# Softmax sums of the second key head: ones-products on TensorE, or accumulating transfers into SBUF

## The chip, the cores and the metric

The kernel runs on one core of a Trainium2 chip. The metric is the device time of one execution in microseconds (us); a kernel's number is the median of several executions. The engines are named as in the profile: PE is TensorE's matmuls, PEld its weight loads, DVE is VectorE, ACT is ScalarE, POOL is GpSimd, SP is SyncE; SPq, ACTq and POOLq are their DMA-issuing instructions.

## What is computed

The input `x` has 8192 rows of 128 channels. A graph layer with the dense 8192 x 8192 matrix `adj` comes first, then a transformer block with causal attention over the 8192 rows (4 query heads of 32 channels, 2 key and value heads, each of which serves 2 query heads), then a mixture of 8 expert networks of which each row uses 2. Cut to what matters here:

```python
x = x + relu(A_norm @ (layernorm(x) @ W.T))          # graph stage, reads adj
h = rmsnorm(layernorm(x), ln1_w)
q, k, v = rotate(h @ wq.T), rotate(h @ wk.T), h @ wv.T
scores = q @ k.T / sqrt(32), causal                   # per query head
att = softmax(scores)                                 # exp(scores - shift) / sum over keys
y = att @ v
x1 = x0 + y @ wo.T                                    # then router, top 2 of 8 experts, result added
```

The part in question is the sum over keys in the softmax: for every query and head, the sum of `exp(scores - shift)` over all keys up to the query's own.

## The kernel before, in words

Three stages run one after the other. `graph_stage` streams `adj` from memory in transfers of 1 MB. `attention_stage` computes attention, the output projection, and the routing of the rows to experts. `expert_stage` runs the experts over the gathered rows and adds the result. The change is in `attention_stage` alone.

Attention works on 16 blocks of 512 queries (`T` = 0 to 15) and, for each, on the `T + 1` blocks of 512 keys that it may see. One pair of a query block and a key block is a **unit**; there are 16 x 17 / 2 = 136, numbered by `first_unit(T) + v`. Within block `T`, `v = 0` is the diagonal unit (masked, with narrower tiles), and `v = 1` to `v = T` are the full ones. A unit has four **chunks** (`j` = 0 to 3) of 128 keys, and in each chunk two **key heads** (`kv` = 0 and 1), each with two query heads.

The work of one chunk, and who does it:

- PE, `scores` (L1234): transposed scores of 128 keys by 2 x 512 queries into `ps_scores[kv]`, two products. There is one such bank pair for each key head, so `scores` for the next chunk waits until ACT has read the last.
- ACT, `exponentials` (L918): `probs[:, j, kv]` = exp of it, 128 x 1024 in float32, one instruction for each key head. `probs` has four chunks and two key heads, exactly one unit; so ACT writes chunk `j` of a unit over chunk `j` of the unit before, and waits until its readers are done: `chunk_used` (PE's products) for both heads, and `chunk_added` (POOL's additions) for key head 0.
- PE, `weigh` (L1245): weights times values into `ps_out`, in four column strips of 32, one for each query head.
- The softmax sums. For key head 0 POOL adds the chunk's `probs` to `chunk_sum` element by element (`add_chunk`, L783 and L786), and once for each query block PE sums `chunk_sum` over its partitions (`combine`, L1273). For key head 1 PE does it all: `add_weights` (L1255) multiplies `probs` of two chunks by a block of ones, in four column strips at once, and adds into `ps_sum`. It runs twice in a unit, after chunks 1 and 3 (after 2 and 3 in a diagonal one).
- PE, `gap`, called four times for each chunk: in a full unit it holds one `max_pass` (L1215), a product whose 128 x 512 result DVE reduces to a row maximum (`reduce_tile`, L958). It is the shift of the next query block, `T + 1`; block 15 has none to prepare. Two banks (`ps_max`) alternate, and a product waits until DVE is done with the one before the last (`bank_free`).

The order of PE's instructions is written out by hand in `unit_of_block`: the scores of chunk `j + 1` are issued ahead of the weighing of chunk `j`, with gaps between. Where a chunk is `paired` (odd, in a full unit), the scores of the two key heads are issued back to back and the gap that would stand between them comes after `weigh`.

Beside this the stage routes rows to experts. DVE, ACT and PE work on it in the gaps; POOL's part (`route`, called after each chunk) are two additions for each query block (L793, L798) and the **scatters** (`scatter_rows`, L810): indirect DMAs of 128 rows of 130 values (66 KB) from `batch_rows` to `scratch_slots`. One is issued after each chunk in units 25 to 32, 48 to 55, 90 to 97 and 128 to 133, 120 in all in 30 units; before it is issued, POOL waits until the scatter before has landed:

```python
                if earlier:
                    pool.wait_ge(rows_scattered, 16 * earlier)
```

All DMAs that POOL issues go to one queue, which the profile lists as q0. In the first 12 units ACT also issues large transfers that fill `scratch_slots` and `scratch_parts` (L860, L868).

Of the kernel before, what the change touches and what calls it, by code (L numbers as in the profile page):

```python
# [25 lines left out]
P = 128  # L26
C = 128
SUB = 4
BT = SUB * P
NH, NKV, HD = 4, 2, 32  # L30
NREP = NH // NKV
# [546 lines left out]
def attention_stage(nc, NB, dram, keep):  # L578
# [10 lines left out]
    PER_CHUNK = NKV  # L589
    EXPS = SUB * PER_CHUNK  # L590
# [10 lines left out]
    first_unit = lambda T: T * (T + 1) // 2  # L601
# [5 lines left out]
    for Rs in batches[:-1]:  # L607
# [4 lines left out]
        paces.append(1 if LAST - 1 in Rs else 2)  # L612
        scattered_at.append(routed_at[-1] + 4 * paces[-1])

    def preparing(unit):

        for R in range(LAST):
            if prepared_at[R] <= unit < prepared_at[R] + 3:
                yield R, unit - prepared_at[R]
# [24 lines left out]
    with ExitStack() as ctx:  # L644
# [4 lines left out]
        q_stack = sb("q_stack", [STACK, QBUF, NH, BT], F16)  # L649
        probs = sb("probs", [P, SUB, NKV, NREP, BT])  # L650
        chunk_sum = sb("chunk_sum", [P, NREP, BT])
        zeros = sb("zeros", [SHIFT_ROW, P], F16)
        even_and_odd = sb("even_and_odd", [P, P])
        unit_max = sb("unit_max", [P, TILES, NB + 1])
# [47 lines left out]
        exp_done = sem("exp_done")  # L702
        chunk_used = sem("chunk_used")
        chunk_added = sem("chunk_added")
        numerator_copied = sem("numerator_copied")
        sums_copied = sem("sums_copied")
        combined = sem("combined")
# [66 lines left out]
        def _(pool):  # L774
            def add_chunk(T, unit, j, diagonal):
# [8 lines left out]
                else:  # L784
                    pool.wait_ge(chunk_added, unit * SUB + j)
                    nc.gpsimd.tensor_tensor(chunk_sum[:, :, lo:], chunk_sum[:, :, lo:], weights, ALU.add  # L786
                                            ).then_inc(chunk_added, 1)

            def divide(R):
                pool.wait_ge(inverted, SUB * (R + 1))  # L790
                pool.wait_ge(numerator_copied, R + 1)
                here = attended[:, R * BT:(R + 1) * BT]
                nc.gpsimd.tensor_tensor(here, here, denominators[:, R % KEPT], ALU.mult).then_inc(block_divided, 1)  # L793
# [47 lines left out]
            for T in range(NB):  # L841
                for n, G in enumerate(units_of(T)):
                    for j in range(SUB):
                        add_chunk(T, first_unit(T) + n, j, n == 0)
                        route(first_unit(T) + n, j)
            divide(LAST)
            keep_residual(LAST)
# [3 lines left out]
        def _(act):  # L851
# [58 lines left out]
            def exponentials(unit, j, diagonal):  # L910
                lo = j * P if diagonal else 0
                for kv in range(NKV):
                    act.wait_ge(scores_ready, unit * EXPS + (PER_CHUNK * j + kv + 1))
                    if unit:
                        act.wait_ge(chunk_used, unit * SUB + (j - SUB + 1))
                        if kv == 0:
                            act.wait_ge(chunk_added, unit * SUB + (j - SUB + 1))
                    nc.scalar.activation(probs[:, j, kv, :, lo:], ps_scores[kv][:, :, lo:], ACT.Exp,  # L918
                                         scale=SCALE).then_inc(exp_done, 1)

# [277 lines left out]
        def _(pe):  # L1198
# [51 lines left out]
            def add_weights(j, diagonal):  # L1250
# [6 lines left out]
                                                start=False, stop=True, skip_group_check=True)  # L1257
                return last

            def clear_sums(T):  # L1260
                if T:
                    pe.wait_ge(sums_kept, T)
                nc.tensor.matmul(ps_sum[:], zeros[:], k_stack[0:SHIFT_ROW, 0, 0:BT], start=True, stop=True,
                                 skip_group_check=True)
# [67 lines left out]
            def unit_of_block(T, v):  # L1332
                unit, G, diagonal = first_unit(T) + v, units_of(T)[v], v == 0
                if diagonal:
                    pe.wait_ge(max_rounded, T + 1)
                    gap(T, v, 0)
                    gap(T, v, 1)
                    pe.wait_ge(shift_placed, T * 16 + 16)
                    for kv in range(NKV):
                        scores(T, unit, G, 0, kv, True)  # L1340
                for j in range(SUB):
                    paired = not diagonal and j % 2
                    for kv in range(NKV):
                        if j + 1 < SUB:
                            scores(T, unit, G, j + 1, kv, diagonal)
                        elif v < T:
                            scores(T, unit + 1, units_of(T)[v + 1], 0, kv, False)
                        if not (diagonal and j == 0) and not (paired and kv == 0):
                            gap(T, v, 4 * j + kv - bool(paired))
                    pe.wait_ge(exp_done, unit * EXPS + PER_CHUNK * (j + 1))  # L1350
                    if diagonal and j == 0 and T:
                        pe.wait_ge(numerator_copied, T)
                    weigh(G, j, diagonal)
                    if paired:
                        gap(T, v, 4 * j + 1)
                    gap(T, v, 4 * j + 2)
                    if diagonal and j == 2:
                        clear_sums(T)
                    if j in ((2, 3) if diagonal else (1, 3)):
                        add_weights(j if j % 2 else j - 1, diagonal).then_inc(chunk_used, 2)  # L1360
                    if diagonal and j == 0 and T:
                        combine(T - 1, lambda: gap(T, v, 3))
                    else:
                        gap(T, v, 4 * j + 3)
# [465 lines left out]
```

## Time and profile before

| | us |
|---|---|
| three runs, median (lowest to highest) | 4142.93 (4135.64 to 4162.34) |
| the profiled execution, own time | 4167.11 |
| its span in the profile | 4165.5 |
| PE busy in the span | 3452.7 (83%) |
| DVE busy | 2752.5 (66%) |
| POOL busy | 1638.8 (39%) |
| ACT busy | 1306.4 (31%) |
| mean granted TensorE clock, share of full speed | 0.911 |

The profiled execution is a single one; its own time is 24.2 us above the median of the three runs, and all durations of the trace are from it. The span is the profile's window from the first to the last instruction. Busy time counts instructions only, not waits; an engine's share over the whole span is a mean over three stages with different limits. The attention stage lies at about 1,500 to 3,680 us of the span.

### The profile page before, as it was taken

The page shows a single profiled execution, that of the slowest core. Times are in us where ns is not written, and L with a number is a line of the kernel's source. Part 1 is how long each engine was busy: PE and PEld are TensorE (multiplying, and loading weights), DVE is VectorE, ACT ScalarE, POOL GpSimd, SP SyncE. Part 2 cuts the span into 40 slices and gives each one's busy share as a digit, 9 for nine tenths or more (in the row PEclk, how much of TensorE's full clock was granted, in tenths as well). Part 3 has the DMA queues.
Part 4 walks back from the last instruction along what each step waited for, and adds up shares of the span by engine and source line. Part 5 has one row for each costly group of instructions (what it writes and reads, how often), then busy time and mean ns, then how long its engine had stood idle before and what let it go on. Part 6 is the DMA issues. An engine that isn't in the chain of part 4 may idle for free. (4 is left out here: it accounts for less than half of the span.)

```text
span 4165.5 us, 48116 instructions
## 1 busy us (share of the span) xinstructions
PE 3452.7 (83%) x16381; PEld 1324.3 (32%) x16381; DVE 2752.5 (66%) x3882; ACT 1306.4 (31%) x1635; POOL 1638.8 (39%) x1016
## 2 busy tenths in 40 slices
PE   1456899999999859987999899999899999839960
PEld 1233444444444312222222222222222222105540
DVE  8778887614344457777778878777777775326752
ACT  0000000000000014433444455454445455625640
POOL 1000000000000014544766486565478566844551
PEclk8567899999999969999999999999999999969985
DMA  9888998787888436500100000000000000012225
GB/s 372 347 346 346 345 344 319 288 292 284 296 296 291 169 123 236 181 10 5 33 13 6 12 21 8 10 1 10 1 23 9 6 1 6 12 54 65 75 65 181
DMA packets 165282, 572.71 MB, mean 137 GB/s; under 512 B 20193, under 2 KB 55786, under 8 KB 114550
## 3 DMA queue, kind: packets, MB, share of 16 engines
q1 hardware_dynamic: 91304, 457.35, 29.7%
q10 hardware_dynamic: 60432, 88.88, 6.0%
q0 software_dynamic: 13360, 24.03, 1.8%
q8 instruction: 113, 1.85, 0.2%
q14 instruction: 73, 0.60, 0.0%
HBM read 478.22 MB, written 90.57 MB: 137 GB/s over the span
## 5 line engine op out<-in xcount | busy, mean ns | idle before, releaser
L958 DVE TENSOR_REDUCE unit_max<-ps_max 128x1 f32<-128x512 f32 (+3 forms) x2176 | 1356.6, 662 | 424.2 <-PE ps_max L1215 306.6
L786 POOL TENSOR_TENSOR chunk_sum<-chunk_sum,probs 128x1024 f32<-128x1024 f32 (+1 forms) x528 | 1196.1, 2265 | 577.4 <-ACT probs L918 563.2
L918 ACT ACTIVATE probs<-ps_scores 128x1024 f32<-128x1024 f32 (+1 forms) x1088 | 1020.9, 984 | 1057.2 <-PE ps_scores L1234 858.4
L1215 PE MATMUL ps_max<-keep_k_stack,q_stack 96*128 96x512 f16 (+3 forms) x2176 | 762.1, 383 | 154.4 <-DVE unit_max L958 114.1
L1234 PE MATMUL ps_scores<-q_stack,keep_k_stack 97*128 97x512 f16 (+3 forms) x2176 | 616.1, 378 | 36.4 <-ACT probs L918 32.6
L1245 PE MATMUL ps_out<-probs,keep_v 128*32 128x512 f32 (+3 forms) x4352 | 567.2, 594 | 0.6 <-ACT probs L918 0.6
L314 DVE TENSOR_TENSOR partial_degree<-partial_degree,ring 128x2048 f32<-128x2048 f32 x240 | 550.0, 2292 | 7.1
L1215 PEld LDWEIGHTS ps_max<-keep_k_stack,q_stack 96*128 96x128 f16 x2176 | 182.2, 97 | 974.8 <-DVE unit_max L958 822.2
L497 PE MATMUL ps_gather<-ring,keep_attended 128*128 128x512 f32 x960 | 449.2, 630 | 22.1 <-DVE keep_attended L338 22.1
L512 PE MATMUL ps_gather_low<-ring,keep_attended 128*128 128x512 f32 x800 | 362.2, 609 | 1.4 <-DVE keep_attended L338 1.4
L277 POOL DMA_DIRECT2D scratch_lower<-lower x15 | 9.3, 618 | 815.7 <-ACT lower L416 815.7
L1234 PEld LDWEIGHTS ps_scores<-q_stack,keep_k_stack 97*128 97x128 f16 x2176 | 208.0, 99 | 325.0 <-ACT probs L918 112.4
L1255 PE MATMUL ps_sum<-probs,keep_ones_heads 128*32 128x512 f32 (+3 forms) x2176 | 295.1, 610 | 0.0
L497 PEld LDWEIGHTS ps_gather<-ring,keep_attended 128*128 128x128 f32 x960 | 193.3, 204 | 263.3 <-issue 263.3
L289 POOL DMA_DIRECT2D keep_k_stack<-k_hi x64 | 31.8, 497 | 577.2 <-DVEq L385 575.2
L1535 POOL DMA_INDIRECT scratch_parts<-moe_y_rows,moe_y_index x156 | 161.6, 1036 | 139.8 <-issue 70.0
L512 PEld LDWEIGHTS ps_gather_low<-ring,keep_attended 128*128 128x128 f32 x800 | 154.2, 196 | 184.5 <-issue 183.0
L481 PE MATMUL ps_gather_low<-ones,partial_degree 128*128 128x1 f32 x512 | 102.4, 334 | 115.9 <-DVEq L333 112.7
L1245 PEld LDWEIGHTS ps_out<-probs,keep_v 128*32 128x32 f32 x4352 | 86.1, 108 | 185.6 <-issue 168.3
L460 PE MATMUL ps_turn<-keep_ident,normed 128*128 128x128 f32 x128 | 25.0, 328 | 138.9 <-DVE normed L329 102.4
L481 PEld LDWEIGHTS ps_gather_low<-ones,partial_degree 128*128 128x128 f32 x512 | 101.1, 306 | 122.7 <-DVEq L333 115.4
L810 POOL DMA_INDIRECT scratch_slots<-batch_rows,keep_slot_index x120 | 118.5, 988 | 36.8 <-POOL chunk_sum L786 16.0
(232 smaller groups left out, 2709.7 us busy)
## 6 DMA issues: line engine op xcount, KB each, us to landing
ring<-in_adj SPq DMA_DIRECT2D x392, 1024.0 KB, 6.7
scratch_slots<-empty_rows ACTq DMA_DIRECT2D x16, 2080.0 KB, 7.4
scratch_parts<-empty_part ACTq DMA_DIRECT2D x8, 2048.0 KB, 7.6
moe_parts<-scratch_parts SPq DMA_DIRECT2D x64, 256.0 KB, 3.5
moe_x_rows<-scratch_slots SPq DMA_DIRECT2D x39, 260.0 KB
x_in<-in_x SPq DMA_DIRECT2D x16, 256.0 KB, 6.0
x_in<-in_x ACTq DMA_DIRECT2D x16, 256.0 KB, 9.9
cos<-in_cos ACTq DMA_DIRECT2D x16, 256.0 KB, 8.0
```

Source lines behind the costliest of these rows:

```text
L314: add = nc.vector.tensor_tensor(partial_degree[:], partial_degree[:], ring[:, g % R, :], ALU.add)
L481: last = nc.tensor.matmul(ps_degree[:, s:s + 1], partial_degree[:, c * BT + s * P:c * BT + (s + 1) * P], ones[:], start=(c == 0), stop=(c ...
L497: last = nc.tensor.matmul(ps_gather[:], support[:, g * SUB + c, :], ring[:, g % R, c * BT:(c + 1) * BT], start=(g == 0 and c == 0), stop=( ...
L512: last = nc.tensor.matmul(bank[:], support[:, g * SUB + c, :], ring[:, slot, c * BT:(c + 1) * BT], start=(start and c == 0), stop=True, sk ...
L786: nc.gpsimd.tensor_tensor(chunk_sum[:, :, lo:], chunk_sum[:, :, lo:], weights, ALU.add).then_inc(chunk_added, 1)
L918: nc.scalar.activation(probs[:, j, kv, :, lo:], ps_scores[kv][:, :, lo:], ACT.Exp, scale=SCALE).then_inc(exp_done, 1)
L958: nc.vector.tensor_reduce(unit_max[:, i, at:at + 1], bank[:, 0:width], AX_X, ALU.max).then_inc(bank_free, 1)
L1215: last = nc.tensor.matmul(out[:, 0:width], q_stack[0:SHIFT_ROW, T % QBUF, h, s * P:(s + 1) * P], k_stack[0:SHIFT_ROW, h // NREP, G * BT:G ...
L1234: last = nc.tensor.matmul(ps_scores[kv][:, r, lo:], keys, q_stack[:, T % QBUF, kv * NREP + r, lo:], start=True, stop=not diagonal)
L1245: last = nc.tensor.matmul(ps_out[h * HD:(h + 1) * HD, lo:], values[:, G * SUB + j, kv * HD:(kv + 1) * HD], probs[:, j, kv, h % NREP, lo:], ...
L1255: last = nc.tensor.matmul(ps_sum[at * HD:(at + 1) * HD, lo:], keep["ones_heads"][:], probs[:, chunk, 1, r, lo:], start=False, stop=True, s ...
L1535: pool.indirect_dma_start(dram[f"parts{s % CHAINS}"], bass.IndirectOffsetOnAxis(y_index[:, g % 2, s:s + 1], 0), y_rows[:, g % 2, s, :], No ...
```

## The change

In the full units but the last of each query block (`v` from 1 to `T - 1`, for `T` from 2 to 15: 105 units), PE's `add_weights` is left out. In its place POOL issues after chunk 1 and after chunk 3 one DMA of two chunks of key head 1, 128 partitions x 2 x 1024 float32 values (1 MB), from `probs` to a new SBUF tile `unit_sums`: in the first such unit of a query block a plain copy, in the others with `accum_op=ALU.add`, which adds to what is there. In the unit `v = T` PE sums `unit_sums` over partitions with the same ones-products (`add_unit_sums`, 2 x 8 products for each query block from 2 on) besides that unit's own `add_weights`.

Three waits come with it. POOL, before a DMA of a pair, waits until the one of the same pair before it has landed (`pair_added[pair]`). ACT, before it writes key head 1 of a chunk, waits until the DMA that reads the old contents has landed. And PE, before `add_unit_sums`, waits for all. `chunk_used` is signalled by `weigh` in the changed units, once a chunk. These units are no longer `paired`, so a `max_pass` stands between the scores of the two key heads in every chunk.

```diff
+    first_added = {}
+    for T in range(NB):
+        for v in range(1, T):
+            first_added[first_unit(T) + v] = v == 1
+    added_before = lambda unit: sum(1 for other in first_added if other < unit)
...
+        unit_sums = sb("unit_sums", [P, SUB, NREP, BT])
...
+            def add_pair(T, unit, pair):
+
+                pool.wait_ge(exp_done, unit * EXPS + PER_CHUNK * (2 * pair + 2))
+                if added_before(unit):
+                    pool.wait_ge(pair_added[pair], 16 * added_before(unit))
+                out, src = unit_sums[:, 2 * pair:2 * pair + 2], probs[:, 2 * pair:2 * pair + 2, 1]
+                out, src = (tile.rearrange("p c r t -> p c (r t)") for tile in (out, src))
+                if first_added[unit]:
+                    if T > 2:
+                        pool.wait_ge(unit_sums_used, T - 2)
+                    pool.dma_start(out, src).then_inc(pair_added[pair], 16)
+                else:
+                    pool.dma_start(out, src, accum_op=ALU.add).then_inc(pair_added[pair], 16)
...
                         add_chunk(T, first_unit(T) + n, j, n == 0)
+                        if first_unit(T) + n in first_added and j % 2:
+                            add_pair(T, first_unit(T) + n, j // 2)
                         route(first_unit(T) + n, j)
...
                         if kv == 0:
                             act.wait_ge(chunk_added, unit * SUB + (j - SUB + 1))
+                        elif unit - 1 in first_added:
+                            act.wait_ge(pair_added[j // 2], 16 * added_before(unit))
...
+            def add_unit_sums(T):
+
+                for pair in range(2):
+                    pe.wait_ge(pair_added[pair], 16 * added_before(first_unit(T) + T))
+                    for half in range(2):
+                        for r in range(NREP):
+                            at = half * NREP + r
+                            last = nc.tensor.matmul(ps_sum[at * HD:(at + 1) * HD, :], keep["ones_heads"][:],
+                                                    unit_sums[:, 2 * pair + half, r, :],
+                                                    start=False, stop=True, skip_group_check=True)
+                last.then_inc(unit_sums_used, 1)
...
-                    paired = not diagonal and j % 2
+                    by_dma = unit in first_added
+                    paired = not diagonal and j % 2 and not by_dma
...
-                    weigh(G, j, diagonal)
+                    last = weigh(G, j, diagonal)
+                    if by_dma:
+                        last.then_inc(chunk_used, 1)
...
-                    if j in ((2, 3) if diagonal else (1, 3)):
+                    if v == T and T > 1 and j == 3:
+                        add_unit_sums(T)
+                    if j in ((2, 3) if diagonal else (1, 3)) and not by_dma:
                         add_weights(j if j % 2 else j - 1, diagonal).then_inc(chunk_used, 2)
```

On POOL, in a unit in which rows are scattered, this is the program of before, for two chunks (L786 is `add_chunk`, L810 the scatter; the waits of an instruction stand in brackets):

```order
L786 TENSOR_TENSOR chunk_sum<-chunk_sum,probs 128x1024 [waits chunk_added,exp_done]
L810 DMA scratch_slots<-batch_rows,keep_slot_index 66048x130 [waits rows_scattered,slots_ready,rows_copied]
L786 TENSOR_TENSOR chunk_sum<-chunk_sum,probs 128x1024 [waits chunk_added,exp_done]
L810 DMA scratch_slots<-batch_rows,keep_slot_index 66048x130 [waits rows_scattered,slots_ready,rows_copied]
L786 TENSOR_TENSOR chunk_sum<-chunk_sum,probs 128x1024 [waits chunk_added,exp_done]
```

and the same two chunks of the changed program, where the lines have moved: L795 is `add_chunk`, L810 now the accumulating transfer of `add_pair`, L833 the scatter.

```order
L795 TENSOR_TENSOR chunk_sum<-chunk_sum,probs 128x1024 [waits chunk_added,exp_done]
L810 DMA unit_sums<-probs 128x2x1024 [waits pair_added0,exp_done]
L833 DMA scratch_slots<-batch_rows,keep_slot_index 66048x130 [waits rows_scattered,slots_ready,rows_copied]
L795 TENSOR_TENSOR chunk_sum<-chunk_sum,probs 128x1024 [waits chunk_added,exp_done]
L833 DMA scratch_slots<-batch_rows,keep_slot_index 66048x130 [waits rows_scattered,slots_ready,rows_copied]
L795 TENSOR_TENSOR chunk_sum<-chunk_sum,probs 128x1024 [waits chunk_added,exp_done]
L810 DMA unit_sums<-probs 128x2x1024 [waits pair_added1,exp_done]
```

The transfer of the pair stands between the addition of the second chunk and its scatter, in the same queue as the scatter; the scatter two rows further down waits, as before, for the scatter that now stands behind the transfer.

On ACT, the exponentials of key head 1 (every second row) in full units of the program of before wait for PE's products and the scores alone:

```order
L918 ACTIVATE probs<-ps_scores 128x1024 [waits chunk_added,chunk_used,scores_ready]
L918 ACTIVATE probs<-ps_scores 128x1024 [waits chunk_used,scores_ready]
L918 ACTIVATE probs<-ps_scores 128x1024 [waits chunk_added,chunk_used,scores_ready]
L918 ACTIVATE probs<-ps_scores 128x1024 [waits chunk_used,scores_ready]
L918 ACTIVATE probs<-ps_scores 128x1024 [waits chunk_added,chunk_used,scores_ready]
L918 ACTIVATE probs<-ps_scores 128x1024 [waits chunk_used,scores_ready]
```

In the changed program, in the same place, they also wait for the landing of the transfers of the unit before:

```order
L945 ACTIVATE probs<-ps_scores 128x1024 [waits chunk_added,chunk_used,scores_ready]
L945 ACTIVATE probs<-ps_scores 128x1024 [waits pair_added0,chunk_used,scores_ready]
L945 ACTIVATE probs<-ps_scores 128x1024 [waits chunk_added,chunk_used,scores_ready]
L945 ACTIVATE probs<-ps_scores 128x1024 [waits pair_added0,chunk_used,scores_ready]
L945 ACTIVATE probs<-ps_scores 128x1024 [waits chunk_added,chunk_used,scores_ready]
L945 ACTIVATE probs<-ps_scores 128x1024 [waits pair_added1,chunk_used,scores_ready]
```

What moved on ACT is nothing; the wait for `pair_added0` or `pair_added1` is new, on key head 1 only.

## Rows read from the trace of the kernel before

**Rows 1.** The page: busy time of each engine over the whole span.

```profile
PE 3452.7 (83%) x16381; PEld 1324.3 (32%) x16381; DVE 2752.5 (66%) x3882; ACT 1306.4 (31%) x1635; POOL 1638.8 (39%) x1016
```

**Rows 2.** Busy time by window; the last two lie in query block 15.

```profile
core 0: us, PE busy (x) PEld busy (x) DVE busy (x) ACT busy (x) POOL busy (x), PEclk, DMA share, GB/s
2700.00:2900.00 200.00, 194.20 (x1168) 55.13 (x1164) 154.92 (x248) 103.61 (x111) 125.61 (x58) 1.00 0.02 6
...
3550.00:3590.00 40.00, 36.34 (x226) 7.88 (x226) 26.11 (x33) 28.34 (x32) 33.12 (x16) 0.96 0.02 6
3600.00:3640.00 40.00, 30.41 (x190) 6.00 (x190) 0.00 (x0) 21.32 (x22) 37.88 (x23) 1.00 0.06 19
```

**Rows 3.** Timeline of one full unit, all engines, tensor clock at full.

```profile
start us, us, engine line op out<-in xcount [idle before <-releaser]
...
2754.47 1.94 ACT L918 ACTIVATE probs<-ps_scores 128x1024 f32<-128x1024 f32 x2 [0.90 <-PE ps_scores L1234]
...
2756.55 1.07 PE L1255 MATMUL ps_sum<-probs,keep_ones_heads 128*32 128x512 f32 x8
...
2757.55 0.39 PE L1215 MATMUL ps_max<-keep_k_stack,q_stack 96*128 96x512 f16 x1
...
2758.41 1.94 ACT L918 ACTIVATE probs<-ps_scores 128x1024 f32<-128x1024 f32 x2 [2.00 <-PE ps_scores L1234]
2758.43 0.60 PE L1234 MATMUL ps_scores<-q_stack,keep_k_stack 97*128 97x512 f16 x2
...
2759.51 2.36 POOL L786 TENSOR_TENSOR chunk_sum<-chunk_sum,probs 128x1024 f32<-128x1024 f32 x1 [1.58 <-ACT probs L918]
...
2761.24 1.94 ACT L918 ACTIVATE probs<-ps_scores 128x1024 f32<-128x1024 f32 x2 [0.90 <-PE ps_scores L1234]
...
2763.32 1.06 PE L1255 MATMUL ps_sum<-probs,keep_ones_heads 128*32 128x512 f32 x8
...
2768.02 1.94 ACT L918 ACTIVATE probs<-ps_scores 128x1024 f32<-128x1024 f32 x2 [0.90 <-PE ps_scores L1234]
```

**Rows 4.** Groups by shape, window 1500:3700, PE (busy us, mean ns).

```profile
L1255 PE MATMUL ps_sum<-probs,keep_ones_heads 128*32 128x512 f32 x1984 | 284.7, 629 | 0.0
```

**Rows 5.** Groups by shape, window 1500:3700, DVE.

```profile
L958 DVE TENSOR_REDUCE unit_max<-ps_max 128x1 f32<-128x512 f32 x1980 | 1282.7, 685 | 313.7 <-PE ps_max L1215 306.6 <-DVE x2T L997 0.2
```

**Rows 6.** Chain of waits, 1500:3700: engine, line, waited for, us, times, longest.

```profile
ACT probs L918 <- PE ps_scores L1234: 858.4, 471, 8.2
...
POOL scratch_slots L810 <- DMA scratch_slots<-batch_rows,keep_slot_index: 13.6, 12, 1.7
```

**Rows 7.** Timeline of POOL, block 15 before its scatters.

```profile
3541.49 17.52 POOL L786 TENSOR_TENSOR chunk_sum<-chunk_sum,probs 128x1024 f32<-128x1024 f32 x7 [2.62 <-ACT probs L918]
```

**Rows 8.** Timeline of POOL, block 15 while it scatters.

```profile
3612.18 0.98 POOL L810 DMA_INDIRECT scratch_slots<-batch_rows,keep_slot_index  x1 [0.17 <-POOL chunk_sum L786]
3613.19 2.38 POOL L786 TENSOR_TENSOR chunk_sum<-chunk_sum,probs 128x1024 f32<-128x1024 f32 x1
3615.73 0.98 POOL L810 DMA_INDIRECT scratch_slots<-batch_rows,keep_slot_index  x1 [0.17 <-POOL chunk_sum L786]
```

**Rows 9.** Timeline of ACT in the same stretch.

```profile
3612.13 1.94 ACT L918 ACTIVATE probs<-ps_scores 128x1024 f32<-128x1024 f32 x2 [1.61 <-POOL chunk_sum L786]
```

**Rows 10.** DMA queues, and issues: KB each, median us to landing.

```profile
q0 software_dynamic: 13360, 24.03, 1.8%
...
ring<-in_adj SPq DMA_DIRECT2D x392, 1024.0 KB, 6.7
scratch_slots<-empty_rows ACTq DMA_DIRECT2D x16, 2080.0 KB, 7.4
...
scratch_slots<-batch_rows,keep_slot_index POOLq DMA_INDIRECT x120, 2.3
```

**Rows 11.** Instructions on scratch_lower: duration ns min/median/max.

```profile
L277 POOL DMA_DIRECT2D scratch_lower<-lower x15: 539/539/1692, 115.1 to 841.2; - x15
...
DMA to landing us min/median/max: 2.3/6.9/9.4
```

More of the change, by code:

```diff
@@ L704, in attention_stage @@
         chunk_added = sem("chunk_added")
+        pair_added = [sem(f"pair_added{n}") for n in range(2)]
+        unit_sums_used = sem("unit_sums_used")
         numerator_copied = sem("numerator_copied")
```

## The prediction

> **What bounds the kernel now.** I read the busy times first, then the windows, then one unit in the timeline, then the chain of waits and the DMA issues. On the page [rows 1] PE is busy 83% of the span, but that is a mean over three stages. The windows [rows 2] show where the change acts: between 2,700 and 2,900 us PE is busy 194 of 200 us at a granted clock of 1.00 (2.4 GHz), DVE 155, POOL 126 and ACT 104. So the full units of most query blocks are bound by PE. Block 15 is different, because it has no `max_pass`: in 3600:3640 POOL is busy 37.9 of 40 us, PE 30.4.
>
> The timeline [rows 3] shows a unit at full clock. ACT starts the two exponentials of chunk 0 at 2754.47 and those of the next unit's chunk 0 at 2768.02: a period of 13.55 us. `add_weights` starts at 2756.55, and the product behind it at 2757.55, so it holds PE for 1.0 us (its eight instructions overlap in four column strips; their mean of 629 ns each [rows 4] must not be multiplied by eight). The chain of waits [rows 6] agrees on who is last: ACT waits 858 us for `ps_scores` from PE.
>
> **The other engines in a unit.** DVE does 16 reductions of 0.685 us [rows 5], 11.0 us. POOL does four additions of about 2.36 us, 9.4 us. Before its scatters, block 15 runs at POOL's own pace: seven additions in 17.52 us [rows 7], 2.50 each, 10.0 us a unit. While it scatters, a chunk costs POOL 3.55 us (3612.18 to 3615.73, with an addition of 2.38 and a scatter of 0.98) [rows 8], 14.2 us a unit, and ACT waits for POOL in each chunk [rows 9].
>
> **What the change removes and adds on PE.** Two `add_weights` a unit, 2 x 1.0 = 2.0 us, so PE's own bound in a changed unit is 11.55 us. `add_unit_sums` puts 2.0 us back in the last unit of each query block: 13 x 2.0 = 26 us for blocks 2 to 14; in block 15 POOL is last and hides it. The moved `max_pass` (no longer paired) keeps four gaps a chunk and is counted as nothing; PE's other work covers it, and if DVE then is late it costs up to the distance from 11.55 to a jittery 12 us, which I put in below.
>
> **What one transfer costs (d).** The trace has no accumulating transfer, and none from SBUF to SBUF of this size. From below: a scatter of 66 KB lands 2.3 us after issue, ACT's fills of 2080 KB after 7.4 [rows 10], so (7.4 - 2.3) / (2080 - 66) = 2.53 us for each further 1000 KB; a plain copy of 1024 KB would land after 4.7 us. The adding transfer has to fetch 2048 KB, source and old sum, so by the same line 2.3 + 0.00253 x 1983 = 7.3 us, of which 5.2 is moving bytes. From above: an adder at half the pace of a copy gives 2.3 + 10.4 = 12.7 us, and no row excludes it. The graph stage's 1 MB loads took 6.7 us in a crowded queue [rows 10], which is of the size of my middle. I take 7.3. Issuing costs POOL 0.54 us, as for the 256 KB store of the graph stage [rows 11]; that is 1.1 us a unit, and twice as much would still fit.
>
> The Trainium skill's page "Collectives: The Full Stack" (section "The bandwidth ceiling: the fold count and why AG ≠ RS ≠ AR") says that an adding transfer is limited by its two source reads on one ring, not by the adder. With the fit of 2.0 us plus bytes over 436 GB/s of the skill's "DMA: Bandwidth & Descriptors" ("Anatomy of one DMA — SWDGE (gpsimd) path"), two reads give an estimate of 6.8 us, and the whole sum below would be +88 instead of +125 us, a time of 4231. No row here shows an adding transfer, so this does not settle d.
>
> **The new wait on ACT.** In [rows 3] chunk 1's exponentials end at 2760.35 and POOL's addition of that chunk at 2761.87, 1.5 us later; only then is the transfer issued. Chunk 0 of key head 1 is written again at 2768.99, 8.64 us after 2760.35, and 7.64 once an `add_weights` between them is gone. Beside that ACT's result may be about 1.0 us late, since ACT would still wait 1.0 of its 2.00 us before chunk 1. So a transfer of d up to 7.64 - 1.52 + 1.02 = 7.1 us is free, and beyond it the period is d + 4.4 us: 11.7 at d = 7.3. Behind the waiting exponential stand the other exponentials, and PE's scores behind them. The transfers themselves need 2 x 5.2 = 10.4 us of each period. With PE (11.55), this wait (11.7), DVE (11.0), POOL (10.5) and the DMAs (10.4) so close, I take 11.9 us.
>
> **The scatters.** This is the largest term. A scatter goes into POOL's one queue (q0 [rows 10]) right behind the pair's transfer. It can land only after it, about 0.4 us later than the transfer. POOL makes one addition and then waits, before the next scatter, for that landing. In the kernel before this wait was rare: 12 times, 13.6 us in all [rows 6]. Now, from the issue of a transfer, it is 7.3 + 0.4 us to the landing, then a scatter, an addition and the gaps, 3.5 us, to the next transfer: 11.2 us for two chunks, 22.4 a unit. What is queued behind is `add_chunk`, for which ACT waits one unit later, and PE behind ACT. Of the 30 scattering units 24 are changed ones: 18 in blocks up to 14, 6 in block 15.
>
> **The sum**, for 105 changed units:
> - 73 units without scatters in blocks 2 to 14: 73 x (11.9 - 13.55) = -120 us.
> - 8 units of block 15 without scatters: the round of exponential, scores, exponential, addition and transfer, 0.97 + 0.63 + 0.97 + 1.52 + 7.3 = 11.4 us, takes the place of POOL's 10.0: +11.
> - 18 scattering units: 18 x (22.4 - 13.55) = +159. 6 in block 15: 6 x (22.4 - 14.2) = +49.
> - `add_unit_sums`: +26.
>
> Together +125 us on the profiled execution's own 4167.1, which would be 4292. That execution is 24.2 us above the median of the three runs, so for a median 4142.9 + 125 = **4268 us**. A measurement of this kernel can tell about 1% from no change.
>
> **The rivals.**
> - *The scatter isn't held up* (its packets pass the transfer's). Then POOL's unit is 4 x 3.55 + 1.1 = 15.3 us: 18 x 1.75 + 6 x 1.1 = +38 in place of +208, the sum -45, 4098 us; with d = 4.7 (11.6 a unit, 73 x -1.95 = -142, and 8 x 1.1 = +9 in block 15) it is -69, 4074. For it speaks that a scatter is small; against it that both stand in one queue, and that POOL did wait 12 times for a landing with nothing but scatters there. This is the rival on the faster side; it decides from the place where the scatter's landing comes less than 4.3 us behind the transfer's issue.
> - *The transfer is fast, the scatter is held up*: d = 4.7. -142 + 9, scattering units 2 x 8.6 = 17.2 us, 18 x 3.65 + 6 x 3.0 = +84, and +26: -23, 4120 us, no change.
> - *The DMA engines become the bound*: d = 10, of which 7.7 moves bytes, makes every changed unit at least 15.4 us: 73 x 1.85 + 8 x 5.4 + 18 x 14.25 + 6 x 13.6 + 26 = +543, 4686 us. At d = 12.7 the unit is 20.8 and the sum +1109, 5252. From 6.8 us of moving on, a changed unit is slower than before even without scatters. Against it speaks that the queues are nearly idle here (a DMA share of 0.02 [rows 2]).
> - *DVE holds PE* at 12.6 us: the first term is -69, the sum +176, 4319; part of the forecast's own case.
>
> **Chances.** Forecast's case, scatters held up and d between 6 and 9: 0.38. Scatter not held up: 0.22. Fast transfer, scatter held up: 0.15. DMA-bound: 0.25. Faster by over 1%: most of the second, 0.19. Within 1%: the third and a rest of the second, 0.18. Slower: 0.63. The range leaves out the fastest end and the slow adder's far end: 4070 to 4720; the likeliest case alone spans 4190 (d = 6) to 4500 (d = 9).
>
> **What would show it.** In the profile after: about 210 transfers `unit_sums<-probs`, landing after some 7.3 us; `add_weights` down from 2176 to 496 records and 224 new ones of `add_unit_sums`; ACT waiting for `unit_sums<-probs` little in plain units and a period near 11.9 us there; POOL waiting for the landing of scatters some 4 us, twice a unit, in units 25 to 32, 48 to 53, 92 to 97 and 128 to 133, and a period near 22 us there. The forecast is wrong if scatters land after 2.3 us as before, if plain units take 13.5 us or more, or if the transfer lands before 5 or after 9 us.

## The result and the profile after

The changed kernel takes 4363.18 us (median of four runs, 4358.54 to 4373.29) against 4147.85 us of the kernel before (median of four, 4135.64 to 4162.34): a ratio of 1.0512, with a 95% interval of 1.0486 to 1.0537. It is slower, as forecast, and by more than forecast: +215 us in the medians and +191 us between the two profiled executions (4358.5 and 4167.1), where the sum said +125. All terms below are from the two profiled executions.

The page of the changed kernel, against [rows 1]:

```profile
PE 3404.8 (78%) x14925; PEld 1294.9 (30%) x14925; DVE 2720.3 (62%) x3882; ACT 1325.2 (30%) x1635; POOL 1877.1 (43%) x1226
```

PE is busy 48 us less and POOL 238 us more. PE's saving is small for 1,456 products taken away, because the others last longer: the 4,352 products of `weigh` are busy for 618 us where they had 567 (642 ns each instead of 594), at a mean granted clock of 0.885 against 0.911. The windows, against [rows 2]:

```profile
core 0: us, PE busy (x) PEld busy (x) DVE busy (x) ACT busy (x) POOL busy (x), PEclk, DMA share, GB/s
2700.00:2900.00 200.00, 187.17 (x1041) 51.87 (x1038) 157.43 (x255) 111.86 (x118) 160.47 (x85) 1.00 0.72 134
3100.00:3300.00 200.00, 152.68 (x746) 40.44 (x746) 119.43 (x190) 75.64 (x82) 130.50 (x82) 0.87 0.45 92
```

The first window holds mostly units without scatters: PE still at a clock of 1.00, ACT with 112 us of work where it had 104, so a little faster than before. In it the DMA engines' share is 0.72, from 0.02. The second holds the scattering units of block 13: PE falls to 153 of 200 us and its clock to 0.87.

The DMA issues and the wait list (window 1500:3900), against [rows 10] and [rows 6]:

```profile
unit_sums<-probs POOLq DMA_DIRECT2D x210, 1024.0 KB, 8.0
...
scratch_slots<-batch_rows,keep_slot_index POOLq DMA_INDIRECT x120, 3.0
```

```profile
ACT probs L945 <- PE ps_scores L1261: 697.9, 438, 7.9
...
ACT probs L945 <- DMA unit_sums<-probs: 355.1, 129, 9.4
...
POOL scratch_slots L833 <- DMA scratch_slots<-batch_rows,keep_slot_index: 183.8, 52, 5.7
```

The wait of POOL for the landing of a scatter grew from 13.6 to 183.8 us; ACT has a new wait of 355 us for the transfers. The instructions that issue the transfers, the copies (L808) and the adding ones (L810), with their landing:

```profile
L808 POOL DMA_DIRECT2D unit_sums<-probs x28: 718/752/776, 1601.4 to 3634.8; - x28
...
DMA to landing us min/median/max: 4.6/4.8/8.4
```

```profile
L810 POOL DMA_DIRECT2D unit_sums<-probs x182: 1172/1197/1662, 1666.9 to 3868.9; - x182
...
DMA to landing us min/median/max: 7.8/8.0/13.6
```

A copy of 1 MB lands after 4.8 us, the adding one after 8.0; the latter also holds POOL for 1.20 us.

**Unit by unit.** ACT's timeline gives the start of each unit's first exponential; the distance to the next is the unit's time. Summed by kind (my table, from the timelines; the forecast's term beside it):

```
units                          count   before    after   difference  forecast
blocks 2-14, no scatters          73   1120.5   1096.5      -24         -120
blocks 2-14, scattering           18    263.5    388.1     +125         +159
block 15, no scatters              8     92.9    112.1      +19          +11
block 15, scattering               6     80.1    133.2      +53          +49
last units of blocks 1-15         15    335.2    366.3      +31          +26
diagonal units                    16    283.8    279.5       -4            0
sum                              136   2176.0   2375.8     +200         +125
```

The rest of the kernel is 8 us shorter in this execution. So four of the five terms came out within 34 us of the forecast, and one is far off: the gain in the 73 units without scatters.

Of these, 27 late ones (59 to 64, 70 to 76, 100 to 103 and 109 to 118) have no routing work and follow no scattering unit; I call them plain units. They take 13.55 us before and 12.69 after, where 11.9 was forecast. A plain unit's chunk in the changed kernel:

```profile
3508.28 0.61 PE L1242 MATMUL ps_max<-keep_k_stack,q_stack 96*128 96x512 f16 x2
...
3508.71 2.52 DVE L985 TENSOR_REDUCE unit_max<-ps_max 128x1 f32<-128x512 f32 x4 [0.63 <-PE ps_max L1242]
3508.72 0.60 PE L1261 MATMUL ps_scores<-q_stack,keep_k_stack 97*128 97x512 f16 x2
...
3509.46 0.39 PE L1242 MATMUL ps_max<-keep_k_stack,q_stack 96*128 96x512 f16 x1
...
3510.43 1.06 PE L1272 MATMUL ps_out<-probs,keep_v 128*32 128x512 f32 x8
...
3511.43 0.61 PE L1242 MATMUL ps_max<-keep_k_stack,q_stack 96*128 96x512 f16 x2
```

The chunk takes 3.15 us (3508.28 to 3511.43). DVE's four reductions take 2.52 us and then it waits 0.63 us for the next product. PE too has a gap: the scores start at 3508.72 and hold PE about 0.44 us (two products of 0.22, as the starts of such pairs show), to 3509.16, and the next max product starts at 3509.46. Neither is full, and in this chunk neither waits for a transfer. In the kernel before, the same group of two max products is followed by `add_weights` in every second chunk, here at 2756.55 [rows 3], and DVE works through both banks beside it and then waits only 0.25 us:

```profile
2756.01 0.61 PE L1215 MATMUL ps_max<-keep_k_stack,q_stack 96*128 96x512 f16 x2
2756.44 1.29 DVE L958 TENSOR_REDUCE unit_max<-ps_max 128x1 f32<-128x512 f32 x2 [0.63 <-PE ps_max L1215]
...
2757.97 2.00 DVE L958 TENSOR_REDUCE unit_max<-ps_max 128x1 f32<-128x512 f32 x3 [0.25 <-PE ps_max L1215]
```

And a pair of chunks in a scattering unit, POOL's timeline, against [rows 8]:

```profile
3241.93 1.35 POOL L810 DMA_DIRECT2D unit_sums<-probs  x1
3243.58 1.03 POOL L833 DMA_INDIRECT scratch_slots<-batch_rows,keep_slot_index  x1 [0.30 <-issue]
...
3244.61 2.39 POOL L795 TENSOR_TENSOR chunk_sum<-chunk_sum,probs 128x1024 f32<-128x1024 f32 x1
...
3251.05 1.00 POOL L833 DMA_INDIRECT scratch_slots<-batch_rows,keep_slot_index  x1 [4.05 <-DMA scratch_slots<-batch_rows,keep_slot_index]
3252.07 2.37 POOL L795 TENSOR_TENSOR chunk_sum<-chunk_sum,probs 128x1024 f32<-128x1024 f32 x1
...
3254.38 1.34 POOL L810 DMA_DIRECT2D unit_sums<-probs  x1
```

This is the step as forecast: transfer, scatter behind it, addition, and then 4.05 us of waiting for that scatter. From transfer to transfer it is 12.45 us, 24.9 a unit (22.4 forecast).

### The profile page after: what moved, and what is told of

Its sections match the earlier page's. It is cut to its first block and busy times, and to the rows that moved or that the text cites. A ratio compares the mean times of both kernels' runs of the same rounds, so it can differ in the third digit from the quotient of the medians.

```text
span 4356.9 us, 45622 instructions
## 1 busy us (share of the span) xinstructions
PE 3404.8 (78%) x14925; PEld 1294.9 (30%) x14925; DVE 2720.3 (62%) x3882; ACT 1325.2 (30%) x1635; POOL 1877.1 (43%) x1226
## 5 line engine op out<-in xcount | busy, mean ns | idle before, releaser
L985 DVE TENSOR_REDUCE unit_max<-ps_max 128x1 f32<-128x512 f32 (+3 forms) x2176 | 1331.5, 660 | 583.5 <-PE ps_max L1242 446.7
L945 ACT ACTIVATE probs<-ps_scores 128x1024 f32<-128x1024 f32 (+1 forms) x1088 | 1042.0, 986 | 1227.5 <-PE ps_scores L1261 697.9
L795 POOL TENSOR_TENSOR chunk_sum<-chunk_sum,probs 128x1024 f32<-128x1024 f32 (+1 forms) x528 | 1244.1, 2356 | 360.3 <-ACT probs L945 348.4
L1242 PE MATMUL ps_max<-keep_k_stack,q_stack 96*128 96x512 f16 (+3 forms) x2176 | 787.1, 395 | 211.3 <-DVE unit_max L985 134.4
L1261 PE MATMUL ps_scores<-q_stack,keep_k_stack 97*128 97x512 f16 (+3 forms) x2176 | 682.7, 398 | 228.0 <-ACT probs L945 227.2
L1272 PE MATMUL ps_out<-probs,keep_v 128*32 128x512 f32 (+3 forms) x4352 | 617.6, 642 | 0.2 <-ACT probs L945 0.2
L810 POOL DMA_DIRECT2D unit_sums<-probs x182 | 224.1, 1231 | 0.0
L833 POOL DMA_INDIRECT scratch_slots<-batch_rows,keep_slot_index x120 | 121.0, 1008 | 208.7 <-DMA scratch_slots<-batch_rows,keep_slot_index 183.8
```

What stands on the lines that cost most here:

```text
L810: pool.dma_start(out, src, accum_op=ALU.add).then_inc(pair_added[pair], 16)
L985: nc.vector.tensor_reduce(unit_max[:, i, at:at + 1], bank[:, 0:width], AX_X, ALU.max).then_inc(bank_free, 1)
L1242: last = nc.tensor.matmul(out[:, 0:width], q_stack[0:SHIFT_ROW, T % QBUF, h, s * P:(s + 1) * P], k_stack[0:SHIFT_ROW, h // NREP, G * BT:G ...
L1261: last = nc.tensor.matmul(ps_scores[kv][:, r, lo:], keys, q_stack[:, T % QBUF, kv * NREP + r, lo:], start=True, stop=not diagonal)
L1272: last = nc.tensor.matmul(ps_out[h * HD:(h + 1) * HD, lo:], values[:, G * SUB + j, kv * HD:(kv + 1) * HD], probs[:, j, kv, h % NREP, lo:], ...
```

## The experiments

"Plain" units and "routing units" (the 28 in which DVE has routing steps, 497 us in all before, 491 in the changed kernel) are read from the timelines as above; a "steady" scattering unit is the mean of units 51 to 53 and 95 to 97 (25.1 us in the changed kernel). The kernel before took 4154 to 4157 us beside these runs (medians of 10 to 13 executions, each spread over some 20 us). The totals of e2, e3, e5, e6, e7 and e10 are single executions.

**e1: no transfers in scattering units.**

```diff
-        for v in range(1, T):
-            first_added[first_unit(T) + v] = v == 1
+        mine = [first_unit(T) + v for v in range(1, T) if first_unit(T) + v not in scattering_units]
+        for unit in mine:
+            first_added[unit] = unit == mine[0]
```

> The changed kernel, but the 24 of its units in which POOL scatters rows keep the products of before; 81 units have transfers. Theory A (scatters queue behind the transfers and POOL waits for their landing): those units fall from 21.6 and 22.2 us to 13.6 to 14.6, the wait of POOL for scatters falls from 184 us to some 14, plain units stay at 12.6; time about 4130 us, a ratio of 0.995 to before. Theory B (the transfers load DMA, POOL and ACT wherever they stand, the scatters don't matter): the loss shrinks with the count of transfers, 24 of 105, from +215 to about +166 us, 4310.

Measured: 4144.12 us, ratio 0.9967 (0.9949 to 0.9984). The 24 units fell from 521 to 343 us in all, as before the change (344), POOL's wait for scatters to 24.8 us in 17 waits, plain units stayed at 12.70. Taking 48 of 210 transfers away took all of the loss: theory A. It doesn't leave a gain of the size that the products removed would suggest: against the kernel before, the 73 units win 40 us, and the last units of the query blocks give back 27 of them and the eight other changed units of block 15 another 10.

**e2: copies in place of the adding transfers.**

```diff
-                    pool.dma_start(out, src, accum_op=ALU.add).then_inc(pair_added[pair], 16)
+                    pool.dma_start(out, src).then_inc(pair_added[pair], 16)
```

> All 210 transfers are plain copies; the accumulation is left out, so the sums of key head 1 lack most units. If the landing of the adding transfer (8.0 us) is what holds a plain unit at 12.6 us and a scattering one at 24.6, then with the copy's 4.8 us a plain unit falls to PE's 11.6 and a scattering one to 2 x 8.7 = 17.4; time about 4110 us. If PE's new order or DVE holds the plain unit, it stays at 12.6 and only the scattering ones fall, about 4170.

Measured: 4202.22 us. All 210 transfers land after a median of 4.7 us. Steady scattering units fell from 25.1 to 18.4 us; there the landing is what counts. The time is 32 us above the 4170 of the second case. The plain unit went to 12.58, only 0.1 lower: the rival won there, and ACT's wait is not what holds plain units.

**e3: small transfers in scattering units.**

```diff
+                if unit in scattering_units:
+                    out, src = out[:, :, 0:64], src[:, :, 0:64]
```

> In the 24 scattering units the transfer moves only 64 of each 1024 values (64 KB in place of 1 MB), so the sums there are incomplete; count, issue and waits stay. Theory A: the scatter is held up by the bytes in front of it; it lands after 2.5 to 3.5 us, these units fall to POOL's own 4 x 3.55 + 2.4 = 16.6 us, time about 4155. Theory C (the adding transfer's own instruction and its wait cost it, whatever its size): they stay above 20 us, time over 4300.

Measured: 4210.23 us. The steady scattering units take 17.3 us, near the 16.6 of POOL's own work, and the wait of POOL for scatters is down to 12.9 us, that of the kernel before (13.6):

```profile
3155.67 1.34 POOL L815 DMA_DIRECT2D unit_sums<-probs  x1
3157.31 1.01 POOL L838 DMA_INDIRECT scratch_slots<-batch_rows,keep_slot_index  x1 [0.30 <-issue]
3158.34 2.36 POOL L798 TENSOR_TENSOR chunk_sum<-chunk_sum,probs 128x1024 f32<-128x1024 f32 x1
3160.87 0.99 POOL L838 DMA_INDIRECT scratch_slots<-batch_rows,keep_slot_index  x1 [0.17 <-POOL chunk_sum L798]
```

The same instructions in the same order, with 1/16 of the bytes: the second scatter starts 3.56 us after the first in place of 7.47. So it is the bytes in front of the scatter in the queue. The time is 55 us above the figure expected, which was that of the kernel before. In the attention stage, against the kernel before, the 24 scattering units take 28 us more, the last units of the blocks 31, and block 15's eight others 12, while the 73 units win only 18: units 34 and 99, behind a batch, took 21.5 and 19.3 us. So in the sum the units behind a batch must be counted with it.

**e4: the transfer ahead of the addition.**

```diff
-                        add_chunk(T, first_unit(T) + n, j, n == 0)
                         if first_unit(T) + n in first_added and j % 2:
                             add_pair(T, first_unit(T) + n, j // 2)
+                        add_chunk(T, first_unit(T) + n, j, n == 0)
```

> The transfer of a pair is issued ahead of the addition of its second chunk, some 1.4 us earlier. If ACT's wait for the landing (landing + 4.4 us) holds a plain unit at 12.6 us, the unit falls by up to 1.0 to PE's 11.6, some -60 us in all; in scattering units the addition now runs beside the transfer, 9.7 us for two chunks in place of 12.3, about -125 us; time about 4165 us. If PE's order or DVE holds plain units, they stay at 12.6 and the time is about 4230.

Measured: 4344.69 us, ratio 1.0456 (1.0437 to 1.0476), a miss. The 24 scattering units did fall, by 72 us in all (steady 20.5 us). Plain units were again at 12.58. But the routing units rose from 491 to 582 us, which neither theory had. The second of the three equal steps of unit 82, DVE, POOL and PE, in e4:

```profile
2992.09 5.28 POOL L795 TENSOR_TENSOR chunk_sum<-chunk_sum,probs 128x1024 f32<-128x1024 f32 x2
2992.15 2.78 DVE L1054 TENSOR_TENSOR newton<-inv_std 128x16 f32<-128x16 f32 x1
...
2995.18 2.22 DVE L1057 SCALAR_TENSOR_TENSOR inv_std<-newton,inv_std 128x16 f32<-128x16 f32 x1
...
2998.18 0.61 PE L1242 MATMUL ps_max<-keep_k_stack,q_stack 96*128 96x512 f16 x1 [5.07 <-DVE unit_max L985]
```

and the same step in the changed kernel:

```profile
3000.93 0.16 DVE L1054 TENSOR_TENSOR newton<-inv_std 128x16 f32<-128x16 f32 x1
```

An operation on 16 values a partition takes 0.16 us with no addition of POOL beside it and 2.78 us when it starts with one. It ends with that addition (the row of 5.28 us is two of them), and the operation at 2995.18 is held in the same way by the second. One addition is enough: in the kernel before, a copy starts 0.01 us after a single addition and ends 0.03 us after it.

```profile
1835.37 2.35 POOL L786 TENSOR_TENSOR chunk_sum<-chunk_sum,probs 128x1024 f32<-128x1024 f32 x1 [0.48 <-ACT probs L918]
1835.38 2.37 DVE L1022 COPY inv_std<-guess 128x16 f32<-128x16 f32 x1
```

Two of them back to back catch two operations of one step. In e4 PE then waits 5.07 us for its bank, and in the window 2970:3100 its granted clock is 0.77 in place of 0.93. Over all routing units the durations of DVE's operations sum to 479 us, where they are 419 in the changed kernel.

**e5, e6: another order of PE.** In the changed units the two gaps of a chunk's scores come behind both scores.

```diff
-                        if not (diagonal and j == 0) and not (paired and kv == 0):
+                        if by_dma and kv:
+                            gap(T, v, 4 * j)
+                            gap(T, v, 4 * j + 1)
+                        elif not by_dma and not (diagonal and j == 0) and not (paired and kv == 0):
```

> Plain copies in place of the adding transfers, as in e2 (the accumulation is left out), and PE's order in the changed units altered: scores of both key heads, two max products, weigh, two max products. Theory P (a plain unit stands at 12.6 us because a max product waits some 0.3 us for its bank in each chunk, the place of two in a row being too near to the next): no such wait is left, the plain unit falls to 11.0 to 11.6 us and the time from 4202 to about 4145 us. Rival (something else than the place of the max products holds it, the chain PE to ACT to PE or POOL): it stays at 12.6.

Measured: 4209.56 us, a miss; plain units 12.36, 0.22 lower than in e2 and far from 11.0 to 11.6, while the routing units took 512 us (493 in e2). PE's wait went to another place:

```profile
2792.05 0.61 PE L1242 MATMUL ps_max<-keep_k_stack,q_stack 96*128 96x512 f16 x2
2792.48 2.59 DVE L985 TENSOR_REDUCE unit_max<-ps_max 128x1 f32<-128x512 f32 x4 [0.50 <-PE ps_max L1242]
...
2793.36 0.85 PE L1242 MATMUL ps_max<-keep_k_stack,q_stack 96*128 96x512 f16 x2
2794.14 1.06 PE L1272 MATMUL ps_out<-probs,keep_v 128*32 128x512 f32 x8
```

Now the second max product ahead of `weigh` waits for a bank, `weigh` starts late, and DVE runs dry (0.50 us) during it.

> The changed kernel with its adding transfers and PE's order of e5. If the landing of the adding transfer (8.0 us after issue) gives its own bound of landing + 4.4 us right behind PE's, a plain unit falls only to about 12.4 us, and the time stays within 4345 to 4360 us. If the landing is no bound near there, it falls as far as in e5, to 11.0 to 11.6, about 4300 us.

Measured: 4383.77 us, and plain units at 12.71 us on average, swinging between 12.34 and 13.3; with copies in the same order (e5) they stand at 12.36. So the adding transfer costs some 0.3 us in this order, as a bound of landing plus 4.4 us right behind the other would; its issue, which holds POOL 0.47 us longer than a copy's, was not separated from that. The routing units lost 39 us and the time is above the range expected; DVE's durations there sum to 442 us (419 in the changed kernel), so part of it goes the way of e4.

**e7: shorter reductions.** On e2, DVE reduces 128 of 512 values.

```diff
-                nc.vector.tensor_reduce(unit_max[:, i, at:at + 1], bank[:, 0:width], AX_X, ALU.max).then_inc(bank_free, 1)
+                nc.vector.tensor_reduce(unit_max[:, i, at:at + 1], bank[:, 0:min(width, P if unit else width)], AX_X, ALU.max).then_inc(bank_free, 1)
```

> The kernel of e2 (plain copies, the accumulation left out), and DVE reduces only 128 of the 512 values of each full max product, so the shifts lack part of the keys. One reduction takes 0.28 in place of 0.66 us. Theory P: banks come back in time, the max products no longer wait and the plain unit falls from 12.6 to PE's own 11.0 to 11.4 us, without a new order. Rival (PE's own work fills 12.6 us): it stays.

Measured: 4058.25 us; plain units at 11.35 us, with PE's instructions and order unchanged from e2's 12.58. A window of e7 (its columns as above: busy time and count of PE, PEld, DVE, ACT and POOL, then clock, DMA share and GB/s):

```profile
2700.00:2750.00 50.00, 48.41 (x290) 14.58 (x287) 18.95 (x64) 28.03 (x31) 33.40 (x18) 1.00 0.32 115
```

PE runs 290 products in 50 us, where e2, in the same window, ran 256 with DVE busy for 40.93 us. Over the 73 units without scatters the gain against e2 is 99 us (1078 to 980). So DVE's reductions hold back 1.2 of the 2.0 us of products removed. That they do it through the turn on two banks is read from the rows of the changed kernel (DVE idle for 0.63 us in each chunk, PE for 0.30); no run has a third bank.

**e8, e9: a kernel faster than both?** e8 joins e1, e5's order, the transfer ahead of the addition in units without routing, and leaves block 15 out.

> A try for a kernel faster than both: transfers only in blocks 2 to 14 and in no scattering unit, PE's order of e5, and the transfer ahead of the addition in units without routing work. By theory A and P the plain units fall to 11.6 to 12.0 us (landing + 3.0, or PE), the scattering ones and block 15 are as before; about 4080 to 4105 us, a ratio of 0.983 to 0.989. If the landing or DVE holds plain units at 12.6, the ratio is 0.995.

Measured: 4146.70 us, ratio 0.9975 (0.9959 to 0.9990), a miss: plain units 12.43, and the routing units 525 us (498 in e1). No better than e1. e9 keeps the addition first and e5's order outside routing units only:

```diff
+                        apart = by_dma and unit not in routed_units
+                        if apart and kv:
```

> Transfers as in e1 (none in scattering units) and none in block 15; PE's order of e5 only in the changed units without routing steps; the transfer behind the addition. The 18 scattering units and block 15 stand as before, the other 73 at 1075 us in all (1080 in e1, some 28 plain units lower by 0.2), the last units of blocks 2 to 14 cost their +26: about 0.992 to 0.995 of before. If block 15's transfers were no loss in e1, no better than e1's 0.9967.

Measured: 4128.43 us against 4155.80, ratio 0.9941 (0.9925 to 0.9957). Routing units 491 us, scattering ones 342. It is 0.6% faster than the kernel before. Its plain units are at 12.74, so e5's order adds nothing with the adding transfers; leaving block 15 alone does (169 us in its 14 full units without the last, from 183 in e1, and 9.5 us in the last, from 21.1).

**e10: e4, with the addition first in routing units.**

> The kernel of e4 (transfer ahead of the addition), but with the addition ahead again in the units that have DVE routing steps. Theory D (two additions of POOL right behind each other hold up DVE's short operations on SBUF, 0.17 to 2.78 us, PE then waits for its bank and its clock falls): the routing units go back from 582 us in all to some 491, and the time from 4345 to about 4255 us. Rival (the early transfer itself, wherever it is, makes ACT and PE late): the routing units fall only in part and the time stays above 4300.

Measured: 4271.97 us; the routing units went back from 582 to 510 us, and DVE's durations in them to 430 us. The edit alone can't tell the two additions in a row from the early transfer in these units, but with DVE's durations it speaks for theory D for most of it; the remaining 19 us were not followed up.

## Why the prediction was right or wrong

- *The direction, and the place of the loss: right.* "POOL makes one addition and then waits, before the next scatter, for that landing." The 24 scattering units cost +178 us (+208 forecast), and e1 and e3 show the cause: without the transfers, or with 1/16 of their bytes, the loss there goes. In the rows above the transfer landed 8.1 us after its issue and the scatter 0.2 us behind it (8.3 in all, 7.7 forecast), POOL began the next scatter 0.8 us after that, and the next transfer 3.3 us later: 12.45 us for two chunks, not 11.2.
- *That this term is below the forecast is partly a matter of which units are counted.* Units 25, 29, 30, 92 and 93 did not stretch; why was not tested. But the loss ran on into units that the sum had elsewhere: 33, 98 and 134, each behind a batch, took 35 us more than before, and 27 and 54, last units that scatter, 18 more. With these it is some 230 us.
- *One transfer: nearly right.* The line from 66 KB to 2080 KB gave 4.7 us for a copy, and 4.7 to 4.8 was measured. For the adding one it gave 7.3, measured 8.0. The issue, which is inside this time, was put at 0.54 us; it took 1.20 us, against 0.73 for a copy, and this 0.47 may be part of the 0.7 missing. The Trainium skill's page "Collectives: The Full Stack" ("The bandwidth ceiling: the fold count and why AG ≠ RS ≠ AR") puts ReduceScatter in a ring, whose add reads two sources, at half of AllGather's rate. Here, for a transfer inside one SBUF, beyond the first 2.3 us the adding transfer took 5.7 us against 2.4 of the copy, 2.4 times, so a little worse than that.
- *The new wait on ACT: right formula, wrong weight.* Landing + 4.4 us gives 12.4 at 8.0, and e6 against e5 fits that bound. But it isn't what holds the plain unit: with copies it stands at 12.58, with adding transfers at 12.69.
- *The step that failed* is "The moved `max_pass` ... is counted as nothing", with DVE's bound put at 11.0 us. DVE's busy time was about right (10.1 us of reductions), its bound wasn't: with two banks PE can be at most two products ahead, and between two groups of max products stands `weigh`, 1.0 us. In the kernel before, `add_weights` stood between max products and DVE caught up beside it. With it gone, PE waits for banks 0.3 us in each chunk, and the unit stops at 12.58. e7 shows that DVE's reductions hold it (11.35 with short ones), and not only in plain units: 99 us over the 73. Of the term's miss of 96 us, 28 are units 33 and 98, the scatters' backlog; 21 are the 27 plain units, 22 the 20 with routing steps, 21 the 20 in which rows are prepared for it.
- *The rival "DVE holds PE at 12.6 us"* gave the mechanism and the number of the plain unit, but I had put it inside my own case and not carried it into the sum. With it the sum would have been +176; measured +191. That these are so close is luck in part: its first term would have been -69, and -24 was measured.
- *The total.* 4363 us lies inside the span of the forecast's likeliest case (4190 to 4500) and 95 us above the forecast's 4268. Between the two profiled executions it is 66 us: the one term's 96, set off in part by the 34 that the scattering units of blocks 2 to 14 stay under theirs.
- *The rivals refuted*: the scatter does not pass the transfer (8.3 us to its landing, and e3); the DMA engines are not the bound, though their share is 0.95 in the window 3480:3580: with copies at far less DMA time the plain unit is nearly the same.
- *Block 15 and `add_unit_sums`.* Block 15's scattering units stand (+53, forecast +49). Of its other eight's +19, 11 are unit 134, behind the scatters; the other seven took +8, near the forecast's 7 x 1.4 = 10. `add_unit_sums` agrees by luck (+31, forecast +26): in six last units with nothing else changed it costs 1.23 us, not 2.0, and 18 of the 31 us are units 27 and 54.
- *A sum in the prediction.* With d = 6.8 and the 73 units still at 11.9 us its terms give +97 us, not +88; neither figure decides anything here.

## What to carry to other kernels

Before a large transfer is put on a queue, look for small transfers on the same queue whose landing an engine waits for: here they landed 6.7 us after their issue in place of 2.3. And the bound of an engine that works through few buffers is not its busy time: what is removed from the other engine may have been the time in which the buffer came back, so look at each side's gap in one period of the timeline before counting the removed work as gain.

## What the runs showed of the hardware

A short DVE operation on SBUF can be held until the end of a POOL addition of 128x1024 that runs beside it: 0.16 to 0.17 us alone, 2.78 us in e4, 2.37 us in the kernel before with a single addition. It was seen on operations with two inputs in SBUF and also on copies and TENSOR_SCALAR with one, but not on all: this reciprocal, 0.38 us after an addition had begun, took its usual 0.25 us.

```profile
1871.21 5.29 POOL L795 TENSOR_TENSOR chunk_sum<-chunk_sum,probs 128x1024 f32<-128x1024 f32 x2
1871.59 0.25 DVE L1071 RECIPROCAL total<-total 128x16 f32<-128x16 f32 x1
```

In the stretch where PE waited for DVE, its granted clock was 0.77 in place of 0.93. The Trainium skill's page "SBUF — State Buffer" ("Who interferes with whom") says that a DVE instruction with two SBUF inputs contends with a GpSimd instruction that reads SBUF; the trace agrees (2.78 us for `newton<-inv_std`). An adding transfer of 1 MB from SBUF to SBUF lands after 8.0 us, a copy after 4.7, and issuing it takes POOL 1.20 us against 0.73. A scatter of 66 KB issued right behind an adding one lands a median of 6.7 us after its own issue, 0.3 us behind the transfer.
